# Gathers of a mixture-of-experts stage on one core: thirteen row buffers and eight tiles of lead, for eight and four

## The reference, cut to what matters

```python
x = _layernorm(x + _L0_xattn_ref(x, ctx_1024, ctx_1024))   # called x2 in the kernel
logits = jnp.einsum('nh,eh->ne', xt, router_w)
probs = jax.nn.softmax(logits, axis=-1)
scores, expert_idx = jax.lax.top_k(probs, 2)
scores = scores / jnp.sum(scores, axis=-1, keepdims=True)
...
h = jnp.einsum('nh,ehd->end', xt, up_proj)              # (8, 256, 512)
hidden = _silu(h[..., :D]) * h[..., D:]
out_e = jnp.einsum('end,edh->enh', hidden, down_proj)   # (8, 256, 256)
out = jnp.einsum('ne,enh->nh', gate, out_e)
x = _layernorm(x + out)
```

## Time and profile before

| what | value |
|---|---|
| runs | 251.42, 251.29, 250.74 us; median 251.29 |
| the profiled execution: its own time | 253.51 us |
| its span, first to last instruction | 251.6 us |
| busy in the span: PE, DVE, ACT, POOL | 209.8, 165.2, 107.0, 150.9 us |
| granted TensorE clock, mean | 0.939 |
| routing's last index to the first transposes of the expert stage | 118 to 122.2 us |
| expert stage on PE | 122.2 to 227.0 us |
| last scatter issued | 228.5 us |
| loads of y_dram | 230.7 to 240.4 us |

### The profile page before, as it was taken

One profiled execution on the slowest core, in us unless ns is written; L12 is line 12 of the kernel. 1 busy time (PEld: TensorE's weight loads), 2 busy tenths in 40 slices (PEclk: granted clock), 3 DMA queues, 4 the chain that ended last, 5 costly groups with the idle time before them and its releaser, 6 DMA issues.

```text
span 251.6 us, 4803 instructions
## 1 busy us (share of the span) xinstructions
PE 209.8 (83%) x1403; PEld 186.0 (74%) x1403; DVE 165.2 (66%) x496; ACT 107.0 (43%) x268; POOL 150.9 (60%) x137
## 2 busy tenths in 40 slices
PE   7857979999999999877899999999999999991000
PEld 7746879889899888876788888887788888870000
DVE  3946688988988788488256565565465655650384
ACT  3251324424523411355255445554454545540094
POOL 0364659668677531056736777767777777643580
PEclk9979999999999999996899999999999999998555
DMA  6954456776775101101222332323333233311995
GB/s 229 398 208 167 108 188 170 246 233 173 238 192 172 42 1 44 43 1 5 84 63 78 110 94 84 101 74 105 105 99 96 73 107 99 101 38 31 416 364 191
DMA packets 17238, 33.78 MB, mean 134 GB/s; under 512 B 4829, under 2 KB 7648, under 8 KB 17216
## 3 DMA queue, kind: packets, MB, share of 16 engines
q1 hardware_dynamic: 12752, 21.78, 26.4%
q0 software_dynamic: 3744, 9.35, 12.7%
q10 hardware_dynamic: 720, 2.36, 2.4%
HBM read 25.08 MB, written 9.32 MB: 137 GB/s over the span
## 4 chain that ended last, share of the span: by engine, by line
PE 43%; DVE 16%; POOL 14%; issue 10%; DMA 10%; ACT 4%; POOLq 1%; SPq 0%; DVEq 0%; ACTq 0%
POOL y_dram L1037 7%; PE p_c L558 6%; POOL keep L1018 6%; PE p_y L474 6%; DMA keep<-x_dram,gather_idx 5%; DMA space<-y_dram 4%; PE p_v L413 3%; PE p_c L431 3%; PE p_v L558 3%; PE p_s L458 3%; PE p_a L493 2%; PE p_r L502 2%; PE p_v L402 2%; PE p_c L402 2%; DVE x L668 2%
## 5 line engine op out<-in xcount | busy, mean ns | idle before, releaser
L1037 POOL DMA_INDIRECT y_dram<-keep,scatter_idx x39 | 39.5, 1013 | 19.4 <-issue 10.1
L1018 POOL DMA_INDIRECT keep<-x_dram,gather_idx x39 | 38.1, 978 | 15.3 <-issue 9.1
L558 PE MATMUL p_c<-w_hi,parts 128*128 x104 | 34.6, 414 | 0.0
L835 DVE TENSOR_TENSOR cs<-p_c,cs 128x256 f32<-128x256 f32 x26 | 11.0, 424 | 25.2 <-ACT cs L947 25.2
L1003 POOL TENSOR_TENSOR w_lo<-keep,w_hi 128x1536 fp32r<-128x1536 f32 (+1 forms) x8 | 27.5, 3439 | 0.0
L935 ACT ACTIVATE parts<-p_y 128x256 fp32r<-128x256 f32 x39 | 15.0, 385 | 27.0 <-PE p_y L584 27.0
L828 DVE TENSOR_TENSOR parts<-p_y,parts 128x256 fp32r<-128x256 f32 x39 | 16.5, 424 | 7.0 <-ACT parts L935 6.6
L994 POOL TENSOR_TENSOR cs<-space,vinv 128x256 f32<-128x256 f32 x16 | 9.5, 616 | 18.9 <-DVE vinv L737 15.3
L474 PE MATMUL p_y<-wo,space 128*128 128x256 f32 x64 | 17.3, 418 | 2.8 <-POOL space L986 2.8
L558 PEld LDWEIGHTS p_c<-w_hi,parts 128*128 128x128 f32 x104 | 17.7, 189 | 2.3
L947 ACT ACTIVATE cs<-p_c 128x256 f32<-128x256 f32 x26 | 10.0, 386 | 20.0 <-PE p_c L558 20.0
(11 more groups left out here) (173 smaller groups left out, 531.3 us busy)
## 6 DMA issues: line engine op xcount, KB each, us to landing
keep<-in_weights SPq DMA_DIRECT2D x8, 768.0 KB, 4.6
space<-in_xT SPq DMA_DIRECT2D x8, 256.0 KB, 3.3
keep<-in_x SPq DMA_DIRECT2D x8, 256.0 KB, 3.3
space<-in_ctxT SPq DMA_DIRECT2D x8, 256.0 KB, 3.4
space<-in_ctxt SPq DMA_DIRECT2D x8, 256.0 KB, 3.3
x_dram<-x SPq DMA_DIRECT2D x8, 256.0 KB, 3.7
space<-y_dram SPq DMA_DIRECT2D x4, 512.0 KB, 7.8
space<-y_dram ACTq DMA_DIRECT2D x4, 512.0 KB, 8.1
```

The lines of the kernel that those rows point to most:

```text
L558: last = nc.tensor.matmul(dst, lhs[:, k, :], w[:].rearrange("p e n -> p (e n)")[:, bass.ds(start + col + k * width, width)], start=(n == 0 ...
L1018: nc.gpsimd.indirect_dma_start(xs[k % HELD], None, x2_dram, bass.IndirectOffsetOnAxis(ap=gather_idx[:, k:k + 1], axis=0)).then_inc(xs_ok[k ...
L1037: nc.gpsimd.indirect_dma_start(y_dram, bass.IndirectOffsetOnAxis(ap=scatter_idx[:, k - 2:k - 1], axis=0), xs[s][:, 0:D], None, bounds_chec ...
```

## The change

Three numbers: 13 row buffers for 8; gathers issued 8 tiles ahead for 4; and before step -1 there are AHEAD - 1 = 7 gathers where RING = 3 stood. RING itself, which PE, DVE and ACT use for their own buffers, stays 3.

```diff
 RING = 3
 ROW = D + TOPK
-HELD = 8
+HELD = 13
+AHEAD = 8
...
             pool.wait_ge(gather_ok, 1)
-            for k in range(RING):
+            for k in range(AHEAD - 1):
                 gather(k)
...
             def tile(k, at, has):
-                if has(4):
-                    gather(k + 4)
+                if has(AHEAD):
+                    gather(k + AHEAD)
                 if k == 2:
                     pool.wait_ge(scatter_ok, 1)
```

## The result

Over 20 runs each, the changed kernel took 250.46 us in the median (248.88 to 251.0), the kernel before 252.56 (250.74 to 254.19). The ratio is 0.991 with a 95% interval of 0.9885 to 0.9935: 1.6 to 2.9 us faster. The first three of the twenty runs of the kernel before, the ones on record ahead of the prediction with their median of 251.29, lay at the low end of what it does. The profiled execution took 250.65 us where that of before took 253.51; its span is 248.7 us, the number that the prediction gave for the span. For the time it gave 248.4 us, 2.1 us less than the median.

A forecast was written before the change was run, and what follows sets the result against it. The prediction took PE in the expert stage, held up by gathers that POOL issued too late, as the bound. 2.9 us off the runs' median of 251.29 us, other parts counted zero, gave 248.4 us; range 247.6 to 250.0 us.

The forecast's parts named there:

- PE's pace: Expert stage, tiles 25 to 33 without stalls: PE takes 2.545 us per tile, so 32 tiles take 81.4 us, not 84.3.
- POOL's schedule: POOL in the expert stage: first scatter at 133.1 us, then 2.605 us per pair, gather 38 at 204.7, last scatter 225.6.
- No wait on a scatter's landing: POOL's three waits go: a gather reuses the buffer of a scatter issued 6.5 us earlier; longest scatter landing 4.7 us.
- The level: Whole kernel's time: the gain was taken off the runs' median of 251.29 us, not the profiled execution's 253.51.
- My range: Time of the changed kernel: 247.6 us (3.7 us of gain) to 250.0 us (1.3 us of gain).
- The size of the gain: Expert stage, tiles 6 to 38: late gathers cost PE 2.9 us, all of it gained by issuing gathers earlier.
- The bounds of 1.8 and 3.8: Gain in us: 1.8 if only POOL's issue times counted, 3.8 if all that PE's weight loads waited were on the path.
- the median landing of 2.8 us: Gather 38, last of the expert stage: assumed to land 2.8 us after issue, the middle of the recorded gather landings.
- B: Rival, part of the gain: runs have fewer long landings, last gather was late by 1.8 us; 249.5 us, chance 0.10.
- C: Rival, no change: without long landings PE would have lost only 0.1 us on gathers; 251.2 us, chance 0.09.
- D: Rival, slower: scatter landings grow beyond 6.5 us and gathers from 13 on wait for them; 253.1 us, chance 0.04.
- 11.6 us of lead: Gather 38 issued at 204.7 us where unstalled PE wants its tile at 216.3, against a landing of 2.8, 4.2 at worst.

The follow-up runs named there:

- the four above: Four profiles of the unchanged kernel before; against the changed kernel's 81.26 us for tiles 6 to 38, late gathers cost 3.0, 3.3, 2.7 and 2.0 us.

## Why the prediction was right or wrong

**The mechanism of the change held, step by step.** PE's pace: 2.539 us per tile measured, 2.545 read. POOL's schedule: first scatter at 133.0 (133.1), gather 38 at 204.6 (204.7), last scatter at 225.5 (225.6). No wait on a scatter's landing, no late gather, 23.2 us from the last scatter to the end where 23.1 were. Landings no shorter than before, and PE waited on none after the first. The span came out at the predicted 248.7 us.

**The level failed.** The step was "I take the 2.9 us off the median", with the sentence that followed, that only the number of long landings could differ between the runs and the profiled execution. Three runs made the median of 251.29; 15 to 29 runs make it 251.95 to 252.8. Of the 2.1 us between forecast (248.4) and median (250.46), 1.3 us are this level (252.56 for 251.29) and 0.8 us the gain (2.1 for 2.9). The profiled execution had stood at 253.51 and I read the 2.2 us between it and the three runs as nothing of weight. It had a low stretch of the clock at 16 us, worth 1.5 us, and late gathers worth 3.0; which of these the three runs were spared is not on record. Taken against the profiled execution's own time, the same 2.9 us would have given 250.6; measured were 250.46 and 250.65. That closeness is partly luck, since 253.51 lay 1.0 us above the median of the kernel before. My range had bounds for the gain and none for the level on which the gain stands; times of the changed kernel alone lie 2.1 us apart.

**The size of the gain was a little high.** 2.9 us is right for the two first profiles. Over five profiles of the kernel before the loss is 2.0 to 3.3 us (the four above and 2.8 with the 11 idle matmuls), 2.8 in the mean; the medians of the changed kernel's two sets give 2.1 and 1.9, and 1.8 with the 11 matmuls in both kernels; the interval of the first reaches 2.9. The bounds of 1.8 and 3.8 held it. Why the runs give less than the profiles stays open.

**One term of the reasoning was mis-sized.** For gather 38 the prediction took the median landing of 2.8 us, in the lower bound, in B and in C; measured were 3.6 to 3.8 in every profile that recorded it. The forecast of 2.9 does not hang on it, as it was read from PE's pace. But it moves the cause: the long landings on the way, at 146 and 205 us, bring the loss forward, and its size at tile 38 is set by POOL's slower pace, by its waits on scatters and by this last landing. Where the packets do harm is mostly the scatters that POOL waits for.

**Rivals.** B, part of the gain, comes nearer in gain (1.8 us for the measured 2.1) than my own number, but not for its reason: it kept POOL's three waits and shortened the last landing to 2.8, and what differs between profiles is the waits. C fell: the runs gained 1.6 to 2.9 us. Its sum was too low in itself, since gather 38 issued at 213.6 and landing after 3.7 leaves PE 1.0 us late and not 0.1. D did not occur in the change and does occur where the loop is closed, at 4.0 us per pair. The page cited for C (the Trainium skill, "Runtime: NRT & Kernel Launch", "Instruction fetch mechanics") calls the cost of crossing a 16 KiB boundary "mostly hidden". The traces do not agree for another queue's DMAs: beside such packets scatters took up to 4.7 us, without them at most 2.9.

**How much of the change was needed.** One more tile of lead with one or two more buffers gave 81.3 to 81.4 us, the changed kernel's time. The prediction had worked out 11.6 us of lead where the longest landing seen is 4.8, and should have said so.

## What to carry to other kernels

When a queue of DMAs issues a little slower than its consumer eats, and the lead is about one landing, a long landing can be paid in full; find the loss from the consumer's own pace in a stretch without stalls, and buy the lead in the issuer's idle time at the start. Give lead and buffers together. Here a scatter issued 6.5 us ahead of the gather that reuses its buffer was never waited for, 3.9 us ahead cost the issuer a wait now and then that the lead covered (12 and 9 buffers), and 1.3 us ahead closed a loop on the landing (8 buffers, lead of five). Take a predicted difference off the execution in which it was measured, and give the level a range of its own when only a few runs are at hand.

## What the runs showed of the hardware that was not expected

- A short stretch at 1.2 GHz behind 2.0 to 2.8 us of idle PE came in nine of 13 executions of code that is the same up to there, and cost up to 1.5 us. In the three profiles with idle matmuls in the gap the clock stayed at 2.4 GHz. With 20 of them the runs lay 0.46 us apart (2.1 without) at mean clocks of 0.943 or more; with 11, three of six runs still had 0.938 or 0.939 and were about 1.1 us longer.
- A scatter took 3.0 us or more only with an instruction packet under way between its issue and its landing (53 of 199, against none of 314), and the long ones moved when idle matmuls moved the packets.
- Gathers of the same 128 x 258 values differ by tile: that of tile 38 took 3.6 to 3.8 us in ten profiles, where the median gather took 2.8 to 3.0.
- 2304 semaphore increments on SP, begun after tile 0's rows at about 131 us, were through at 271.00 us: 61 ns each.
- With eight buffers and a lead of five, a gather that waits for a scatter starts 2.72 us after that scatter, where the median landing is 2.5 us: 0.2 us more from the landing to the waiting engine.
